# Strassen's seven products in the last projection of a transformer layer, in eight rounds of 256 rows

## What is computed

```
h = jax.nn.silu(g) * u                        # [2048, 2752]
y = jnp.einsum('bsi,hi->bsh', h, Wd)          # Wd: [1024, 2752]
x = x + _layernorm(y, axis=-1)
```

## Time and profile before

| | us |
|---|---|
| median of three runs | 2738.34 (2737.36 to 2738.40) |
| the profiled execution, its own time | 2737.43 |
| its span, first to last instruction | 2735.7 |
| PE busy | 2630.3 (96%) |
| DVE busy | 1611.1 (59%) |
| ACT busy | 953.0 (35%) |
| POOL busy | 1161.4 (42%) |
| last stage, first matmul to end of span | 2271.7 to 2735.7 |

### The profile page before, as it was taken

One profiled execution on the slowest core, in us unless ns is written; L12 is line 12 of the kernel. 1 busy time (PEld: TensorE's weight loads), 2 busy tenths in 40 slices (PEclk: granted clock), 3 DMA queues, 4 the chain that ended last, 5 costly groups with the idle time before them and its releaser, 6 DMA issues. The chain is left out here.

```text
span 2735.7 us, 42054 instructions
## 1 busy us (share of the span) xinstructions
PE 2630.3 (96%) x17032; PEld 1113.9 (41%) x17032; DVE 1611.1 (59%) x1993; ACT 953.0 (35%) x1676; POOL 1161.4 (42%) x641
## 2 busy tenths in 40 slices
PE   6999899999999999999988989999999999999998
PEld 3445533333333333324544434444444444444443
DVE  6331777778787777735677788777777760101001
ACT  3111266666666666672112223222222220000000
POOL 0000177777777777781222333555555540100001
PEclk9999999999999999999999999999999999999999
DMA  4223101011010110002232332333333327332220
GB/s 173 81 77 94 34 17 30 17 42 34 17 30 17 30 46 17 1 1 108 96 118 86 118 103 73 110 112 103 104 115 116 116 87 270 113 115 72 72 72 31
DMA packets 180383, 209.93 MB, mean 77 GB/s; under 512 B 17652, under 2 KB 138740, under 8 KB 180212
## 3 DMA queue, kind: packets, MB, share of 16 engines
q1 hardware_dynamic: 175440, 198.11, 22.3%
q10 hardware_dynamic: 4772, 9.44, 0.9%
HBM read 146.28 MB, written 61.08 MB: 76 GB/s over the span
## 5 line engine op out<-in xcount | busy, mean ns | idle before, releaser
L791 POOL TENSOR_TENSOR c_prob<-c_prob 128x1024 f32<-128x1024 f32 (+1 forms) x285 | 600.6, 2127 | 517.5 <-ACT c_prob L654 515.0
L673 DVE TENSOR_REDUCE c_maxes<-c_s 128x2 f32<-128x1024 f32 (+3 forms) x640 | 645.8, 1058 | 198.7 <-PE c_s L503 198.7
L654 ACT ACTIVATE c_prob<-c_s 128x512 f32<-128x512 f32 (+1 forms) x1152 | 598.0, 571 | 300.2 <-PE c_s L525 184.9
L525 PE MATMUL c_s<-c_q,c_k 97*128 97x512 f16 (+3 forms) x1280 | 367.3, 353 | 10.1 <-ACT c_prob L654 1.7
L1356 PE MATMUL e_ps<-x_hi,c_hi 128*128 128x512 f16 x832 | 316.8, 381 | 13.4 <-DVE c_hi L1431 10.5
L1357 PE MATMUL e_ps<-x_lo,c_hi 128*128 128x512 f16 x832 | 316.6, 381 | 0.0
L1358 PE MATMUL e_ps<-x_hi,c_hi 128*128 128x512 f16 x832 | 316.6, 381 | 0.0
L540 PE MATMUL c_ctx<-c_prob,v_sb 128*32 128x512 f32 (+3 forms) x2560 | 293.7, 540 | 0.2 <-ACT c_c L638 0.2
L1743 POOL TENSOR_TENSOR c_lo<-c_lo 128x1024 f32<-128x1024 f32 (+2 forms) x66 | 158.4, 2401 | 251.2 <-DVE c_lo L1415 251.2
L525 PEld LDWEIGHTS c_s<-c_q,c_k 97*128 97x128 f16 x1280 | 111.3, 97 | 345.9 <-ACT c_prob L654 299.4
L80 DVE BATCH_NORM_STATS2 f_norm_stats<-f_yp 128x6 f32<-128x512 f32 x16 | 11.2, 699 | 408.6 <-PE f_yp L1963 408.6
(11 more groups left out here) (196 smaller groups left out, 3902.9 us busy)
## 6 DMA issues: line engine op xcount, KB each, us to landing
h_hi<-e_hh SPq DMA_DIRECT2D x84, 128.0 KB, 1.9
h_lo<-e_hl SPq DMA_DIRECT2D x84, 128.0 KB, 1.7
b_x<-L_attn_x SPq DMA_DIRECT2D x16, 512.0 KB, 6.6
c_q<-qk_hi SPq DMA_DIRECT2D x64, 128.0 KB, 3.0
d_x<-L_attn_x SPq DMA_DIRECT2D x16, 512.0 KB, 5.2
x_dram<-d_x SPq DMA_DIRECT2D x16, 512.0 KB, 2.6
f_x<-x_dram SPq DMA_DIRECT2D x8, 1024.0 KB, 7.1
out<-f_z SPq DMA_DIRECT2D x8, 1024.0 KB, 5.0
```

The source lines that it names most:

```text
L525: last = nc.tensor.matmul(S2[:, h % 2, at:at + w], K[:, g % 2, k * P:(k + 1) * P], Q[:, g % 2, b, h, q:q + w], start=True, stop=not diag)
L654: nc.scalar.activation(prob(g, s, 0, w)[:, h, :], S2[:, h % 2, 0:w], ACT.Exp, scale=exp_scale).then_inc(exp_done, 1)
L673: last = nc.vector.tensor_reduce(MAXES[:, g % 2, t // TPB, heads, t % TPB, u], S1[:, heads, at:at + w], AX.X, ALU.max)
L791: return nc.gpsimd.tensor_tensor(one, one, two, ALU.add)
```

## The change

The last stage runs in eight rounds of 256 rows, unrolled. The first two (`PLAIN` = 2) are plain: both tiles advance chunk by chunk, the even round in banks 0 to 3 and the odd one in banks 4 to 7, 260 matmuls each. From the third on, the 16 chunks 4 to 19 are taken in eight pairs (j). With A the rows (two tiles by even and odd chunk) and B the weights (even and odd chunk by left and right half), Strassen's scheme in Winograd's form gives the four output quarters with seven products of 8 x 3 matmuls instead of eight; chunks 0 to 3, 20 and 21 stay plain (D11, D22, D21, D12: 17 matmuls each). P2, P4 and P3 go on in the banks of D11, D21 and D12.

The sums of weights T1 to T4 are made once. T1 to T3 are made by VectorE and cut by ScalarE and VectorE beside the first round; T4 is made beside the second and is written over the weights' right half of the even chunk, so its cut waits until the second round has used the pair (`used`). The sums of rows S1 to S4 are made in every round from the third on, in two groups of four pairs, from both parts of h (`make_sums`), then cut. The products are joined by VectorE in eight steps (`join`) into Z in SBUF, from which the norm is then taken. Rows h now have one buffer of 256 rows: for the plain rounds and the third they are loaded in parts, each when the round before has used the chunks, the last part when its last product is done; from the fourth on chunks 0 to 3, 20 and 21 are loaded after D12, the pairs' even and odd chunks after the sums and P1, and after P4. x has one buffer too. Each tile of 128 rows is stored by itself. The down weights are cut with scale 256 (`GS`), h with 4 (`HS`), so that the sums fit f16.

The core of the diff (only new lines from the fourth piece on; the helpers that name tiles and count semaphores are left out; `t_of`, `s_of`, `a_of`, `b_of` give the hi and lo part of T, S, A, B of pair j):

```diff
-HS = 16.0
+HS = 4.0
...
-                nc.vector.scalar_tensor_tensor(DL[0:n, 0:planes, :], W[0:n, i, 0:planes, :], WS, DH[0:n, 0:planes, :],
+                nc.vector.scalar_tensor_tensor(DL[0:n, 0:planes, :], W[0:n, i, 0:planes, :], GS, DH[0:n, 0:planes, :],
...
-                nc.scalar.activation(DH[0:n, 0:planes, :], W[0:n, tasks[k][1], 0:planes, :], ACT.Copy, scale=WS
+                nc.scalar.activation(DH[0:n, 0:planes, :], W[0:n, tasks[k][1], 0:planes, :], ACT.Copy, scale=GS
...
+    ROUNDS, PLAIN = T // BLOCK, 2
+    MOST = T * c_hi.shape[1] // D
+    PAIRED = slice(FIRST, FIRST + MOST)
+    NJ, GROUP = MOST // 2, BANK // P
+    GROUPED = NJ // GROUP
+    direct = [c for c in range(FULL + 1) if not PAIRED.start <= c < PAIRED.stop]
+    parts = [(FIRST, 8), (8, 12), (12, 16), (16, FULL)]
...
+        return ["0", "1"] if r < PLAIN else ["D11", "D22", "D21", "D12", "P1", "P2", "P4", "P6", "P7", "P5", "P3"]
+    def joins(r):
+        return [] if r < PLAIN else ["11", "U2", "U3", "21", "22", "U4", "22+", "12"]
...
+    banks = {"P1": 0, "D11": 1, "P2": 1, "D21": 2, "P4": 2, "D22": 3, "D12": 4, "P3": 4, "P6": 5, "P7": 6, "P5": 7}
+    last_reader = {"D11": "11", "D21": "21", "D22": "22+", "D12": "12", "P6": "U2", "P7": "U3", "P5": "U4"}
+    S_ORDER = (1, 2, 4, 3)
...
+            for r in range(PLAIN + 1):
+                for i, (start, end) in enumerate(parts):
+                    if r:
                         if end == FULL:
+                            sp.wait_ge(product, product_no[r - 1, "1"])
+                        else:
+                            sp.wait_ge(used, NJ * (r - 1) + (end - FIRST) // 2)
+                    load_chunks(r, start, end, part_loaded[i])
+                    if end == FULL:
+                        load_rest(r, part_loaded[i])
+                if r == 0:
+                    load_x(0)
+                else:
+                    if r == 1:
+                        load_chunks(PLAIN, 0, FIRST, direct_loaded)
+                    store(r - 1)
+                    load_x(r)
+            for r in range(PLAIN, ROUNDS):
+                if r > PLAIN:
+                    store(r - 1)
+                    load_x(r)
+                if r + 1 < ROUNDS:
+                    sp.wait_ge(product, product_no[r, "D12"])
+                    load_chunks(r + 1, 0, FIRST, direct_loaded)
+                    load_chunks(r + 1, FULL - 1, FULL, direct_loaded)
+                    load_rest(r + 1, direct_loaded)
+                    sp.wait_ge(made, s_no(r, GROUPED - 1, 3))
+                    sp.wait_ge(product, product_no[r, "P1"])
+                    load_parity(r + 1, 0, pairs_loaded)
+                    sp.wait_ge(product, product_no[r, "P4"])
+                    load_parity(r + 1, 1, pairs_loaded)
+            store(ROUNDS - 1)
+            sp.wait_ge(stored, 16 * 2 * ROUNDS)
...
+            def bank_free(r, name):
+                if r == PLAIN:
+                    pe.wait_ge(normed, 2 * (r - 1) if banks[name] < 4 else 2 * r)
+                elif name == "P1":
+                    pe.wait_ge(copied, r - PLAIN)
+                elif name in last_reader:
+                    pe.wait_ge(joined, join_no[r - 1, last_reader[name]])
+            def unpaired(r, name):
+                s, n = int(name[1]) - 1, int(name[2]) - 1
+                bank_free(r, name)
+                at = slice(s * P, (s + 1) * P)
+                for c in direct[:-1]:
+                    chunk(bank(name), [h[:, c, at] for h in H], columns(c, n), c == 0, False)
+                rest(bank(name), H[0][:, FULL, at], columns(FULL, n), name == "D22").then_inc(product, 1)
+            def paired(r, name, a, b, opening):
+                if opening:
+                    bank_free(r, name)
+                for j in range(NJ):
+                    last = chunk(bank(name), a(j), b(j), opening and j == 0, j == NJ - 1)
+                last.then_inc(product, 1)
+            def strassen(r):
+                pe.wait_ge(direct_loaded, 32 + 96 * (r - PLAIN))
+                if r == PLAIN:
+                    pe.wait_ge(*part_rows(len(parts) - 1, FULL, r))
+                for name in ("D11", "D22", "D21", "D12"):
+                    unpaired(r, name)
+                if r == PLAIN:
+                    for i, (_, end) in enumerate(parts[:-1]):
+                        pe.wait_ge(*part_rows(i, end, r))
                 else:
+                    pe.wait_ge(pairs_loaded, 64 * (r - PLAIN))
+                paired(r, "P1", lambda j: a_of(j, 0, 0), lambda j: b_of(j, 0, 0), True)
+                paired(r, "P2", lambda j: a_of(j, 0, 1), lambda j: b_of(j, 1, 0), False)
+                pe.wait_ge(cut_lo, t_no(4, NJ - 1))
+                paired(r, "P4", lambda j: a_of(j, 1, 1), lambda j: t_of(j, 4), False)
+                pe.wait_ge(cut_lo, s_no(r, GROUPED - 1, 2))
+                paired(r, "P6", lambda j: s_of(j, 2), lambda j: t_of(j, 2), True)
+                pe.wait_ge(cut_lo, s_no(r, GROUPED - 1, 3))
+                paired(r, "P7", lambda j: s_of(j, 3), lambda j: t_of(j, 3), True)
+                paired(r, "P5", lambda j: s_of(j, 1), lambda j: t_of(j, 1), True)
+                paired(r, "P3", lambda j: s_of(j, 4), lambda j: b_of(j, 1, 1), False)
+            for r in range(ROUNDS):
+                (plain if r < PLAIN else strassen)(r)
...
+            def make_t1_to_t3(j):
+                (b11, l11), (b12, l12), (b22, l22) = b_of(j, 0, 0), b_of(j, 0, 1), b_of(j, 1, 1)
+                t1, t2, t3 = (t_sum(i, j) for i in (1, 2, 3))
+                for i, (start, end) in enumerate(parts):
+                    if start == FIRST + 2 * j:
+                        dve.wait_ge(w_loaded[i], 16 * (6 if end == FULL else 2))
+                if j:
+                    dve.wait_ge(cut_lo, t_no(3, j - 1))
+                tt(t1, b12, b11, ALU.subtract).then_inc(part, 1)
+                tt(t2, l12, l11, ALU.subtract).then_inc(part, 1)
+                dve.wait_ge(part, 5 * j + 2)
+                tt(t1, t1, t2, ALU.add).then_inc(made, 1)
+                dve.wait_ge(made, t_no(1, j))
+                tt(t2, b22, t1, ALU.subtract).then_inc(part, 1)
+                tt(t3, b22, b12, ALU.subtract).then_inc(part, 1)
+                dve.wait_ge(part, 5 * j + 4)
+                tt(t2, t2, l22, ALU.add).then_inc(made, 1)
+                cut_t(1, j)
...
+            def make_sums(r, g):
+                (a11, l11), (a12, l12), (a21, l21), (a22, l22) = (a_group(g, s, odd) for s in range(2) for odd in range(2))
+                s1, s2, s4, s3 = (s_sum(i) for i in S_ORDER)
+                before = s_no(r, g, 1) - 1
+                seen = 7 * NJ + (before // 4 - NJ) * 6
+                dve.wait_ge(cut_lo, before)
+                tt(s1, a21, a22, ALU.add).then_inc(part, 1)
+                tt(s2, l21, l22, ALU.add).then_inc(part, 1)
+                dve.wait_ge(part, seen + 2)
+                tt(s1, s1, s2, ALU.add).then_inc(made, 1)
+                dve.wait_ge(made, before + 1)
+                tt(s2, s1, a11, ALU.subtract).then_inc(part, 1)
+                dve.wait_ge(part, seen + 3)
+                tt(s2, s2, l11, ALU.subtract).then_inc(made, 1)
+                dve.wait_ge(made, before + 2)
+                tt(s4, a12, s2, ALU.subtract).then_inc(part, 1)
+                dve.wait_ge(part, seen + 4)
+                tt(s4, s4, l12, ALU.add).then_inc(made, 1)
+                cut_s(r, g, 1)
+                dve.wait_ge(cut_lo, before + 1)
+                tt(s3, a11, a21, ALU.subtract).then_inc(part, 1)
+                cut_s(r, g, 2)
+                dve.wait_ge(cut_lo, before + 2)
+                tt(s2, l11, l21, ALU.subtract).then_inc(part, 1)
+                dve.wait_ge(part, seen + 6)
+                tt(s3, s3, s2, ALU.add).then_inc(made, 1)
+                cut_s(r, g, 4)
+                cut_s(r, g, 3)
...
+                of, with_, out = {"11": ("P2", P1, Z[:, 0, half[0]]), "U2": ("P6", P1, U2), "U3": ("P7", U2, U3),
+                                  "21": ("P4", U3, Z[:, 1, half[0]]), "22": ("P5", U3, Z[:, 1, half[1]]),
+                                  "U4": ("P5", U2, U2), "22+": ("D22", Z[:, 1, half[1]], Z[:, 1, half[1]]),
+                                  "12": ("P3", U2, Z[:, 0, half[1]])}[name]
+                no = join_no[r, name]
+                if name == "11":
+                    dve.wait_ge(copied, r - PLAIN + 1)
+                    dve.wait_ge(cut_lo, s_no(r, GROUPED - 1, 3))
+                    dve.wait_ge(stored, 16 * 2 * r)
+                if no > 1:
+                    dve.wait_ge(joined, no - 1)
+                dve.wait_ge(product, product_no[r, of])
+                tt(out, bank(of), with_, ALU.add).then_inc(joined, 1)
...
+            for j in range(NJ):
+                make_t1_to_t3(j)
+            normalise_plain(0)
+            for j in range(NJ):
+                make_t4(j)
+                if j % 2:
+                    cut_t(4, j - 1)
+                    cut_t(4, j)
```

(76 more changed lines are left out.)

229 lines of the change are left out of this document (122 added, 107 removed).

## The result

| | before | after |
|---|---|---|
| median of five runs, us | 2738.34 (2737.36 to 2738.84) | 2722.81 (2720.99 to 2723.09) |
| ratio to before, 95% interval | | 0.9943 (0.9931 to 0.9954) |
| the profiled execution, its own time | 2737.43 | 2721.11 |
| its span | 2735.7 | 2719.3 |
| first to last matmul start of the last stage | 450.6 | 436.15 |

The change gains 15.5 us. The sign was right; 9.6 us of the forecast gain, over a third, are missing.

The account below looks back on a forecast made before the run. The last stage was taken to be bound by TensorE's row of matmuls. -31.1 (matmuls) + 4.5 (bubble) + 2.2 (clock) - 0.7 (tail) = -25.1 us, giving a median of 2713.2 us; range 2708 to 2722.

Parts of the forecast that it names:

- Matmuls removed: Last stage, six Strassen rounds: 236 matmuls instead of 260 each, 144 saved at 0.2158 us, 31.1 us gained.
- First round: First round's late weights arrive in time, margin 1.4 us at the 49th matmul; cost 0, at most 3 us.
- The sentence on the later parts: First round: later parts, 2.6 MB, take 7.6 us at 346 GB/s while TensorE takes 10.4 us for them.
- Rival B: First round starves: with equal bytes per queue the first late weights land at 2287, costing 3 us, 2716; chance 0.08.
- Third round, the bubble: Third round's start: TensorE waits for the last part of the rows, 4.5 us, bounds 3.0 and 6.4.
- Its clock: Half clock of TensorE after the third round's bubble, 2.2 us lost, bounds 0 and 2.6.
- Sums of weights: VectorE makes T1 to T3 by 2358 and T4 by 2390, beside the plain rounds; cost 0, margin 7.
- Sums of rows: Every later round: S2 is ready at 26.2, P6 needs it at 30.2; cost 0, margin 4.0 us.
- A: Rival: the weights' sums are late, so S2 in the third round is too; 2719; chance 0.10.
- C: Rival: small waits in each Strassen round, 2 us each, at P6, a bank or the loads; 12 us, 2725; chance 0.06.
- D: Rival: VectorE's chain from last join to S2's cut becomes the bound and eats the gain, up to about 2800; chance 0.04.
- Tail: After the last matmul: join +0.7, first add 0.5 earlier, shorter last store, adds +0.5; together -0.7, bounds -1.5 and 0.

Follow-up runs that it names:

- p8_plain: Changed kernel with `PLAIN` = 8: all eight rounds of 256 rows plain, 2080 matmuls, no sums or joins; 2744.46 us, ratio 1.0028.
- e1_spread: Changed kernel, doubled last weight rows loaded by two transfers of 64 partitions instead of one with outermost dimension 2; 2712.70 us, ratio 0.9910.
- e4_first: Changed kernel, the two weight transfers with outermost dimension 2 issued by ACT ahead of all other weights, not last; 2727.49 us, ratio 0.9961.
- b_spread: Kernel before the change, doubled weight rows loaded by transfers of 64 partitions instead of one with outermost dimension 2; 2737.44 us, ratio 1.0001.
- e5_keep: Changed kernel with unread matmuls ahead of the waits: 26 in the first round's gap, 20 in the third round's; 2717.05 us, ratio 0.9924.
- dve4: Changed kernel with four more dependent VectorE operations (2.9 us) ahead of the row sums of each Strassen round; 2721.85 us, ratio 0.9946.
- dve16: Changed kernel with sixteen more dependent VectorE operations (11.5 us) ahead of the row sums of each Strassen round; 2764.77 us, ratio 1.0107.

## Why the prediction was wrong, point by point

**What bounds the stage: right.** The stage is as long as its row of matmuls, 0.2158 apart as before, and the account closes to 0.1 us.

**Matmuls removed, -31.1: right**, by the round distance of 50.94 and by `p8_plain`.

**First round, "Cost 0, at most 3 us": this step failed, by 8.9 us.** The first late part came in time, as said. The sentence on the later parts charged a load by its bytes at 346 GB/s. That is a rate at which all 16 engines were busy (a DMA share of 1.15 in the earlier trace rows). The rest load has two, and 49 GB/s: its 256 KB for `f_wd_end_lo` and the 256 KB for `f_wd_end_hi` ahead of it on the same engines need 512 KB / 49 GB/s = 10.7 us even if nothing else is on them, and until about 2312 they carry their share of the full loads too. The sentence also took the last part for four chunks, 2.6 MB. It is chunks 16 to 20 and the rest, some 3.9 MB, so 11 us at 346 GB/s and not 7.6, more than TensorE's 10.4; the slack of the parts ahead would have covered that, and in `e1_spread` it did. Rival B had a wait for the first round's weights, but at the first late part (the 49th matmul, 2287) and not at the last, by another mechanism (equal bytes for both queues), and at a third of the size. The trace of before had a sign of this transfer, and of its price too, though nobody waited for it: the earlier trace rows show its issue, and this window of the kernel before has the same trail.

```profile
2314.00:2316.00 2.00, 2.00 (x11) 0.94 (x10) 0.00 (x0) 0.00 (x0) 0.00 (x0) 1.00 0.13 50
```

What should have made me look is that the change moves its deadline forward by some 40 us, and that its access pattern is unlike all others in the stage. The rows I had chosen didn't have this window. `e1_spread`, `e4_first` and `b_spread` show the cause.

**Third round, the bubble of 4.5: right.** It was 4.71 from slot end to start. SP's issue came 0.2 us after the slot's end (forecast 0.35), and the last of the four was issued 1.5 us later:

```profile
2393.88 0.36 SPq L1995 DMA_DIRECT2D f_h_hi<-h_hi  x1
...
2395.42 0.60 SPq L1991 DMA_DIRECT2D f_h_hi<-h_lo  x1
```

**Its clock, 2.2 with a bound of 2.6: too small by 0.7.** The price was 2.90, outside the bound. I had placed it between two neighbours by the length of the gap (1.9 after 5.2 us, 2.6 after 3.8). Over all gaps of these traces the length doesn't set it: 2.2 to 2.9 after gaps of 4.7 to 4.8 us, 2.7 to 2.9 after 6.1 to 6.3, 1.4 to 2.7 after gaps of 6.8 to 6.9, 2.6 after 13.7, and 1.9 to 2.0 after the 5.2 us that every run has at the stage's start. `e5_keep` shows that the price is real and separable, not what sets its size.

**Sums of weights, cost 0: right.** No TensorE wait for `f_t_lo` is there. T1 to T3 end at 2357 (forecast 2358), the norm of round 0 at 2363 (2364), T4 at 2391 (2390). The last agreement is luck: VectorE had finished all but the last cut of T4 at 2387.6, and this one waited until TensorE, late by the first gap, had used the last pair.

**Sums of rows, cost 0, margin 4.0: right.** The lines are from the fourth round, whose t = 0 is 2452.23: GpSimd's two adds, VectorE's first two sums beside them, the same first two sums of the second group without them, the last cut of S2, and TensorE's first matmul of P6.

```profile
2456.92 5.53 POOL L2317 TENSOR_TENSOR f_z<-f_x,f_z 128x1024 f32<-128x1024 f32 x2 [53.65 <-DVE f_z L96]
...
2457.41 2.84 DVE L2191 TENSOR_TENSOR f_sums<-f_h_hi 128x512 f32<-128x512 f16 x1
2460.17 2.83 DVE L2192 TENSOR_TENSOR f_sums<-f_h_lo 128x512 f32<-128x512 f16 x1
...
2472.05 0.68 DVE L2192 TENSOR_TENSOR f_sums<-f_h_lo 128x512 f32<-128x512 f16 x1
...
2477.61 0.68 DVE L2183 TENSOR_TENSOR f_s_lo<-f_sums,f_s_hi 128x512 f16<-128x512 f32 x1
...
2482.45 0.38 PE L2054 MATMUL f_ps<-f_t_hi,f_s_hi 128*128 128x512 f16 x1
```

The hold-up by GpSimd is there: two operations of 2.84 and 2.83 us instead of 0.68, 4.3 us in all, where 4.7 were charged. S2 is cut at 2478.3, so t = 26.1 (forecast 26.2), and P6 starts at t = 30.2: 4.2 us of margin. In the third round the margin was 12.4 and not 6: S2 was cut 3 us later than forecast (2419.1), but P6 came 8.8 later (2431.5), by the first gap. Rivals A, C and D had no part in the result; `dve4` and `dve16` show from which point D would have had one.

**Tail, -0.7: right as a number**, 12.4 against 13.1, but the prediction's own four terms (+0.7, -0.5, -1.9, +0.5) add up to -1.2, and it gives no reason for the -0.7. The passes begin 0.8 us later after the last slot than before (the join). The first add starts 0.95 us after the passes' start (forecast 0.8), where it was 1.42 by the earlier trace rows and not 1.34: -0.5. The adds take 5.07 and not 4.64: +0.4. The last store saves 1.4 and not 1.9. These four make -0.7.

```profile
2710.30 1.54 DVE L96 TENSOR_SCALAR f_z<-f_z,f_norm_mv,f_norm_rstd 128x1024 f32<-128x1024 f32 x2
...
2711.25 5.07 POOL L2317 TENSOR_TENSOR f_z<-f_x,f_z 128x1024 f32<-128x1024 f32 x2 [44.19 <-DVE f_z L96]
2714.05 2.63 SPq L2012 DMA_DIRECT2D out<-f_z  x2
```

**The sum, corrected.** -31.1 + 8.9 (charged 0) + 4.7 (4.5) + 2.9 (2.2) - 0.7 (0.7) = -15.3; measured -15.5. Nearly all of the miss is one term.

**The range.** Its upper end was made of rivals that each cost at most 12 us with a small chance, and of bounds that had no row for a transfer on few engines. A term "at most 3" whose transfer had never been waited for was not bounded from above by any row.

## What to carry to other kernels

When a change moves a deadline forward, list every transfer that ends ahead of the new deadline and price each by its own access pattern; the bulk rate (346 GB/s in the rows of before) didn't hold for the broadcast over an outer dimension of 2, which ran at 49 GB/s here. A transfer that nobody waits for has no wait in the trace of before, so look at its shape, and for a trail in the DMA share: 0.13 stood there. Look too at which reader a wait protects: this one stood 12.9 us ahead of the chunk that reads the load. Price each idle gap of TensorE with 1.4 to 2.9 us of half clock on top (the gaps here were 4.7 to 13.7 us long; behind the 0.7 and 0.3 us of `e5_keep` there was none), and count gaps rather than idle microseconds: five short waits cost 9.9 us of clock in `dve16`.

## What the runs showed of the hardware that I had not expected

- A load on two DMA engines at the head of the queue made TensorE wait 13.5 us for a full load behind it (`e4_first`), more than the 5.9 us that it cost at the end of the queue.
- The half clock behind a gap cost between 1.4 and 2.9 us with no visible relation to the gap's length (4.7 to 13.7 us). The same place of the program gave different prices too: 2.17 in `e1_spread` and 2.90 in the changed kernel behind the same bubble. What sets it stays open.
- Matmuls without a use kept the clock at full speed through a wait, with 0.7 and 0.3 us of idleness left (`e5_keep`): 46 of them shortened the stage by 5.3 us. The two gaps were 0.4 us longer in sum; whether the extra matmuls did that isn't shown.
- While a GpSimd add on 128x1024 ran, a VectorE sum took 2.84 us instead of 0.68, and the add grew as well: the two adds took 5.53 us in the fourth round, 6.74 in the fifth, 4.65 in the kernel before. The slowdown goes both ways. It isn't an even one: each sum that was held up ended some 0.55 us after the end of an add (2460.25 and 2459.70, for example), as if it had waited for it. In the fifth round the first two sums took 0.69 us beside the first add, which then took 3.98, and the third and fourth took 2.72 each. What decides who waits stays open.
